# Decoder kernel on one core: the first expert tile's rows gathered by TensorE with a matrix of ones

## The reference, cut to what matters

```python
h = _layernorm(x, ln_w, ln_b)
logits = h @ router_w
expert_idx = jnp.argmax(logits, axis=-1)
for e in range(E):
    gv = h @ expert_wv[e]
    gate_raw, value = jnp.split(gv, 2, axis=-1)
    y = gate_raw * jax.nn.sigmoid(gate_raw) * value @ expert_proj[e]
    out = out + jnp.where((expert_idx == e)[..., None], y, 0.0)
```

## Time and profile before

| | |
|---|---|
| median of 3 runs | 2994.42 us (2988.17, 2994.42, 2995.18) |
| the profiled execution: its time, its span | 2993.08 us, 2990.6 us |
| busy share of the span | PE 79%, PEld 40%, DVE 65%, ACT 60%, POOL 44% |
| mean granted TensorE clock | 0.92 of full speed |
| the 16 scatters on POOL | first at 2352.19 us, last at 2371.32 us |
| rows loaded back, x_rows<-xs, 19 loads | 128 KB each, 2.0 us to landing |

### The profile page before, as it was taken

The page is one execution under the profiler, slowest core; times in us unless marked ns, Lnnn a source line. Parts: engine busy times, 40 slices in busy tenths (PEclk is TensorE's granted clock), DMA queues, the critical chain, the costliest instruction groups (busy, mean ns, idle before and its releaser), DMA issues. The chain is left out here.

```text
span 2990.6 us, 38704 instructions
## 1 busy us (share of the span) xinstructions
PE 2374.3 (79%) x12420; PEld 1200.4 (40%) x12421; DVE 1957.9 (65%) x1762; ACT 1794.5 (60%) x2789; POOL 1311.3 (44%) x492
## 2 busy tenths in 40 slices
PE   5688888888868888888877667797787499868778
PEld 2344444444334444444435123223222355545333
DVE  4699999999669999999964657515913122233440
ACT  4799999999479999999951440270064211122330
POOL 2089998999508999999951110000000300020000
PEclk8899999999989999999996889898889699979889
DMA  2320001000133000100000400010012400010000
GB/s 77 90 76 28 25 29 39 28 25 28 41 88 77 28 25 29 39 28 28 25 20 3 113 36 1 9 40 11 1 34 88 174 21 21 20 43 9 28 0 28
DMA packets 59817, 116.17 MB, mean 39 GB/s; under 512 B 13619, under 2 KB 21811, under 8 KB 58304
## 3 DMA queue, kind: packets, MB, share of 16 engines
q1 hardware_dynamic: 51104, 103.72, 11.0%
q0 software_dynamic: 8608, 11.05, 1.3%
HBM read 86.92 MB, written 27.53 MB: 38 GB/s over the span
## 5 line engine op out<-in xcount | busy, mean ns | idle before, releaser
L838 POOL TENSOR_TENSOR hs<-hs,c_bc 128x2048 f32<-128x2048 f32 x256 | 1166.3, 4556 | 63.9 <-DVE hs L889 48.6
L889 DVE TENSOR_TENSOR_SCAN hs<-decays,ps 128x512 f32<-128x512 f32 x512 | 610.8, 1215 | 26.4 <-PE ps L916 8.0
L889 DVE TENSOR_TENSOR_SCAN hs<-decays,carry,ps 128x512 f32<-128x512 f32 x512 | 621.7, 1270 | 8.5 <-PE ps L916 7.7
L924 PE MATMUL ps<-hs,sel 128*64 128x512 f32 x2048 | 498.4, 608 | 15.4 <-POOL hs L838 15.1
L916 PE MATMUL ps<-ident,dbu_even 128*128 128x128 f32 x2048 | 294.9, 283 | 94.8 <-DVE hs L889 65.8
L916 PE MATMUL ps<-ident,dbu_odd 128*128 128x128 f32 x2048 | 294.9, 283 | 91.5 <-DVE hs L889 60.5
L852 ACT ACTIVATE decays<-delta_far,A 128x512 f32<-128x512 f32 x512 | 358.2, 712 | 10.3 <-DVE hs L889 10.2
L852 ACT ACTIVATE decays<-delta_near,A 128x512 f32<-128x512 f32 x512 | 356.4, 707 | 3.2 <-DVE hs L889 3.2
L860 ACT ACTIVATE dbu_odd<-du_turned,b_turned 128x512 f32<-128x512 f32 x512 | 357.1, 710 | 0.0
L860 ACT ACTIVATE dbu_even<-du_turned,b_turned 128x512 f32<-128x512 f32 x496 | 346.0, 710 | 0.0
L916 PEld LDWEIGHTS ps<-ident,dbu_odd 128*128 128x128 f32 x2048 | 221.1, 142 | 241.4 <-DVE hs L889 188.0
(11 more groups left out here) (260 smaller groups left out, 2664.3 us busy)
## 6 DMA issues: line engine op xcount, KB each, us to landing
c_bc<-c_rows SPq DMA_DIRECT2D x256, 128.0 KB, 2.8
o_rows<-osb SPq DMA_DIRECT2D x32, 256.0 KB
u_rows<-u SPq DMA_DIRECT2D x4, 1024.0 KB, 4.5
d_rows<-delta SPq DMA_DIRECT2D x4, 1024.0 KB, 4.2
delta_near<-d_rows SPq DMA_DIRECT2D x4, 1024.0 KB, 9.8
hs<-u_rows SPq DMA_DIRECT2D x4, 1024.0 KB, 6.5
delta_far<-d_rows SPq DMA_DIRECT2D x4, 1024.0 KB, 12.1
w_down<-in_expert_proj SPq DMA_DIRECT2D x1, 4096.0 KB, 36.6
```

What stands on the lines that cost most here:

```text
L838: pool.tensor_tensor(x, x, spread(c_bc[:, g, :], 4), ALU.mult).then_inc(weighed.sem, 1)
L889: dve.tensor_tensor_scan(hs[:, quad % RING, n, :], decays[:, s % RING, :], ps[:, DBU + s % RING, :], carry[:, at(i * GB, g), blk] if q els ...
L924: mm = pe.matmul(ps[lo:lo + DB, ACC + quad % 2 * 2 + j // 2, :], k.sel2[:, :], hs[:, quad % RING, j, :], start=False, stop=False, skip_gro ...
```

## The change

For tile 0 alone the way through DRAM is left out. VectorE builds 16 matrices `lands[:, t, :]` of 128x128 float32: a one where token row p of tile t has slot n, for slots 0 to 127, from `slot_f` and a row of the numbers 0 to 127 (`places`) that is loaded with `tile_counts`, which grows from 17.5 KB to 81.5 KB. TensorE sums, over the 16 tiles, rows times lands to the PSUM bank XT, which gives tile 0 channels first, and signals x_turned; this comes ahead of the wait for the weights. The load of tile 0 from `xs` and its `turn_x` are gone; the scatter of all 16 tiles and the other 18 loads stay. `slot_f` lives on past sort_tokens.

```diff
-        counts = k.sb("tile_counts", [P, TT + NT], ctx=ctx)
+        counts = k.sb("tile_counts", [P, TT + NT + P], ctx=ctx)
         slot = k.sb("slot", [P, TT], I32, ctx=ctx)
+        slot_f = k.sb("slot_f", [P, TT], ctx=ctx)
...
-            run_tiles(k, wv, wp, rows, slot, expert, weights_in, NT, c2)
+            run_tiles(k, wv, wp, rows, slot, slot_f, counts[:, TT + NT:], expert, weights_in, NT, c2)
...
+    lands = k.sb("lands", [P, N // P, P], ctx=ctx)
+    landed = k.sig("landed")
...
         def _(sp):
             def body(tile, p):
 
-                tile.wait(sp, x_turned, 1, -1)
-                sp.dma_start(xrow[:, p, :], k.xs[bass.ds(tile.times(P), P), :]).then_inc(x_here[p].sem, 16)
+                if tile.i is not None or tile.c:
+                    tile.wait(sp, x_turned, 1, -1)
+                    sp.dma_start(xrow[:, p, :], k.xs[bass.ds(tile.times(P), P), :]).then_inc(x_here[p].sem, 16)
...
             def turn_x(tile, p):
-                tile.wait(pe, x_here[p], 8, 16 - 8 * p)
+                tile.wait(pe, x_here[p], 8, 8 * p)
...
+            def first_x():
+
+                for c in range(C):
+                    for t in range(N // P):
+                        if c == 0:
+                            pe.wait_ge(landed.sem, landed.at(t + 1))
+                        mm = pe.matmul(ps[:, XT, c * P:(c + 1) * P], rows[:, t, c * P:(c + 1) * P], lands[:, t, :],
+                                       start=(t == 0), stop=(t == N // P - 1))
                 mm.then_inc(x_turned.sem, 1)
...
+            first_x()
             pe.wait_ge(weights_in.sem, weights_in.at(32))
             first = Beat(None, 0)
             e = experts_of(first, FIRST + 1)
-            turn_x(first, 0)
             gate_value(first, 0, 0, e[0])
...
+            for t in range(N // P):
+                dve.tensor_scalar(lands[:, t, :], places, slot_f[:, t:t + 1], None, ALU.is_equal).then_inc(landed.sem, 1)
             all_tiles(dve, body)
...
-        x_here[p].passed(16 * ((NT + 1 - p) // 2))
+        x_here[p].passed(16 * ((NT - 1 + p) // 2))
...
-    a["tile_counts"] = np.tile(np.concatenate([np.arange(N // P) * P, np.arange(N // P + E_ - 1)]).astype(np.float32),
-                               (P, 1))
+    a["tile_counts"] = np.tile(np.concatenate([np.arange(N // P) * P, np.arange(N // P + E_ - 1), np.arange(P)])
+                               .astype(np.float32), (P, 1))
```

More of the change, by code:

```diff
@@ L1371, in experts @@
              later=[(wv[:], a["expert_wv"]), (wp[:], a["expert_proj"])], later_in=weights_in)
-        sort_tokens(k, X, H2, HN, wr, before, counts, rows, slot, expert)
+        sort_tokens(k, X, H2, HN, wr, before, counts, rows, slot, slot_f, expert)
         with ExitStack() as c2:
-            run_tiles(k, wv, wp, rows, slot, expert, weights_in, NT, c2)
+            run_tiles(k, wv, wp, rows, slot, slot_f, counts[:, TT + NT:], expert, weights_in, NT, c2)
         weights_in.passed(32)
@@ L1407, in experts, with sort_tokens @@
         added.passed(NCH)
-def sort_tokens(k, X, H2, HN, wr, before, counts, rows, slot, expert):
+def sort_tokens(k, X, H2, HN, wr, before, counts, rows, slot, slot_f, expert):
     nc, ps = k.nc, k.ps
@@ L1425, in sort_tokens @@
         place = k.sb("place", [P, E_, TT], ctx=ctx)
-        slot_f = k.sb("slot_f", [P, TT], ctx=ctx)
         past = k.sb("past", [1, NT, E_ - 1], ctx=ctx)
@@ L1547, in next, with run_tiles @@
         return Beat(self.i, self.c + n)
-def run_tiles(k, wv, wp, rows, slot, expert, weights_in, NT, ctx):
+def run_tiles(k, wv, wp, rows, slot, slot_f, places, expert, weights_in, NT, ctx):
     nc, ps = k.nc, k.ps
@@ L1618, in turn_x @@
                                       k.ident[:])
+                mm.then_inc(x_turned.sem, 1)
+            def first_x():
[5 more added lines that the diff above has]
+                                       start=(t == 0), stop=(t == N // P - 1))
                 mm.then_inc(x_turned.sem, 1)
@@ L1723, in body @@
                                       1.0, None, ALU.mult).then_inc(hid_copied.sem, 1)
+            for t in range(N // P):
+                dve.tensor_scalar(lands[:, t, :], places, slot_f[:, t:t + 1], None, ALU.is_equal).then_inc(landed.sem, 1)
             all_tiles(dve, body)
+    landed.passed(N // P)
     scattered.passed(16 * (N // P))
     for p in range(2):
-        x_here[p].passed(16 * ((NT + 1 - p) // 2))
+        x_here[p].passed(16 * ((NT - 1 + p) // 2))
         y_stored[p].passed(16 * ((NT + 1 - p) // 2))
```

## The result

Median 2986.88 us (11 runs, 2985.16 to 2991.40) against 2994.15 before (11 runs): 7.3 us by the medians. The ratio of all runs is 0.9978, 95% interval 0.9969 to 0.9987, so 6.6 us (4 to 9) faster, and within 0.3%. The profiled execution took 2986.88 us, its span is 2984.4.

The account below looks back on a forecast made before the run. PE bounds the tile loop; before it, PE waits on the scatter chain. Gain 8.3 us less 0.1 for the larger load is 8.2, so 2993.08 - 8.2 = 2984.9 us; range 2980.5 to 2990.5.

Parts of the forecast that it names:

- What moves out of the path: Between the scatter's landing and tile 1's turn_x, PE's tile 0 work drops out; gain 8.32 us, 8.2 after all edits.
- DVE: Beside the scatter, sixteen 128x128 comparisons at 0.24 us each, starting like POOL, take 3.8 us, over at 2356.0.
- PE's sums: During the scatter, 64 instructions from 2352.45, clock rising after 6 us, are over at 2362.9.
- The register reads: Four reads after first_x, no longer hidden in a wait; unpriced, covered up to the 4.9 us PE waits.
- The clock at the restart: When tile 1 starts at 2375.78, the clock has fallen after PE's 4.9 us wait; costs 3.07 us.
- Rival 1: At tile 1's restart the clock is up; gain 10.0 us, or 11.3 if held throughout; chance 0.15.
- tile_counts: Its load brings 64 KB more, so the norm's block ends 0.12 us later.
- Rival 2: In the scatter, POOL stands still for all of DVE's 3.8 us; gain 4.4 us, time 2988.7; chance 0.19.
- Rival 3: Beside the scatter, each comparison waits for a POOL issue; tile 1's turn_x 4.1 us later, time 2997.3; chance 0.04.
- The signs: Listed as showing it wrong: comparisons over 0.3 us, stretched issues, last scatter after 2371.4, clock 1.00, SP's load after 2373.9.
- a shift of the loop shifts the end by as much: Behind the tile loop everything is serial, so the loop's whole gain of about 8.3 us reaches the end.

Follow-up runs that it names:

- before_warm_long: Kernel before, plus 205 idle identity transposes on PE ahead of the wait for the weights; ratio to before 1.0000, and 0.9996 when repeated.
- keep_busy: Changed kernel plus 50 idle identity transposes between tile 0's turn_hidden and tile 1's turn_x; ratio to before 0.9969, and 0.9957 when repeated.
- compare_wide: Changed kernel plus 12 unused VectorE comparisons of 128x1024 behind the sixteen; a single run, stage 306.74 us, no ratio given.
- compare_slow: Changed kernel with an unused 128x1024 VectorE comparison ahead of each of the sixteen; ratio to before 0.9978.
- change_again: The changed kernel run again, unedited; median 2987.45 us, ratio to before 0.9980.
- before_warm: Kernel before, plus 180 idle identity transposes on PE ahead of the wait for the weights; ratio to before 1.0004.

## Why the prediction was right, point by point

The time lay in the range, 2.0 us above the forecast of 2984.9, and on the side of "within 0.3%", which had 0.53. The point of the forecast itself lay just on the other side, at 0.32%, as it says.

- **What moves out of the path: right.** 8.2 us forecast, 8.19 of stage measured; to tile 2's turn_x it is 8.20. before_warm_long priced tile 0's part by itself at 8.42, against "about 8.4".
- **DVE:** 3.36 us for sixteen, 3.8 forecast. It began 0.76 us ahead of POOL, not with it, so only one issue was lengthened.
- **PE's sums:** 9.04 us, over at 2361.3; 10.4 forecast. The clock was up about 3.5 us after the start, sooner than the 6 taken. Nothing hung on it: the wait only became longer, 6.6 us instead of 4.9.
- **The register reads**, which no row priced: PE stood still for 1.01 us between its sums of rows and the gate sums, instead of 0.57 between turn_x and the gate sums, so they cost at most 0.44, covered as said.
- **The clock at the restart: right.** It was down, having fallen 3.0 us after PE stopped, inside the 4.9 us of the forecast; t1 to t2 took 15.19, against 12.24 + 3.07 = 15.31 forecast. keep_busy showed the cause. Rival 1's upper end, 11.3 us with the clock held throughout, is what keep_busy reaches: 11.2 of stage.
- **tile_counts:** 0.12 us forecast, nothing measured: from the norm's first load to the router's first matmul it is 23.92 us before and after.
- **Rival 2** was real but 30 times smaller: 0.12 us on one issue, not 3.8. An issue is lengthened beside VectorE, it does not stand still until VectorE is done: in compare_wide by 0.31 to 0.40 us, in compare_slow by 0.45. By the Trainium skill (SBUF — State Buffer, Who interferes with whom) a VectorE instruction in a two-port mode and a GpSimd instruction exclude each other for a whole instruction; as an estimate from that rule and the 0.75 us measured, an issue of compare_wide could lose up to 0.75 us to each instruction that it meets. The measured loss stays below that; no run shows the ports or the mode.
- **Rival 3's** price was wrong. At 0.86 us a comparison its sum gives tile 1 at 2384.6 (2366.0 + 18.6), and it stood at 2379.5: the sum kept the clock down through the second pass and half the gate sums, and in compare_slow it rose within the second pass.
- **The signs:** two of those named for rivals 2 and 3 came although neither rival held, the last scatter at 2371.91 (later than 2371.4) and SyncE's first load at 2374.34 (later than 2373.9). They were given as times of the span: 0.45 us of the delay is the stage's own later start, 0.14 is left.
- **The step that failed:** "a shift of the loop shifts the end by as much". The serial part behind held 1.5 us longer in the profile, 2.7 in change_again. 1.4 of it is each time the fall of the clock in the linear attention shown above; the other 1.3 in change_again were not traced to a line. That, and the norm's block beginning 0.45 us later, which no edit explains (it differs as much between runs without the change), is the difference between 8.2 and 6.2 of span. The intervals of the ratio alone (4 to 9 us, and 3 to 9) don't show this loss, they reach to 8.2 and beyond; it rests on the profiled executions.

## What to carry to other kernels

Work that fills a wait is free only as far as the engine behind it restarts as before: here the wait that was left over cost 3 us behind it, since TensorE came out of it at half clock. So after moving work into a wait, look at the granted clock where the wait ends, and fill the remainder, with useful work if there is some, with idle transposes if not; the waits of 1.1 us that keep_busy and before_warm_long left did no harm, after the 2.9 us of before_warm the idle work had gained nothing. And price a moved part at full clock, then ask separately who pays the slow start. A stage far behind, whose code is untouched, can pay one too.

## What the runs showed of the hardware that was not expected

- PE idling 2.9 us was enough to find the gate sums at half clock, though the granted clock was 1.00 until 0.2 us before the restart (before_warm); 0.95 to 1.13 us were not (keep_busy, before_warm_long, each twice). After a wait of 1.9 us the clock fell in four executions of thirteen, and only once PE was at work again.
- POOL's indirect issue goes from 0.96 to 1.08 us beside 128x128 tensor_scalar instructions of VectorE, to 1.27 beside 128x1024 ones (1.36 for the first), and to 1.41 beside a mixture of both.
- Behind the 205 transposes the first load came 0.8 us later after POOL's last issue than behind 180, twice, with one packet on the instruction queue in the window; that the one causes the other isn't shown.
- The clock of a later, untouched stage differed between kernels and repeated in both runs of a kernel, 2.2 us of time: a difference of that size, end to end, says little of an edit.
